# Bucket stage of a two-layer graph network: VectorE's fold of the last bucket is put between the first and the second comparison

## What is computed

```python
h1 = relu(x[row] @ nbW + nbb); h2 = relu(x[col] @ selfW + selfb)
log_alpha = concatenate([h1, h2]) @ attW + attb
gate = sigmoid(log(u) - log1p(-u) + log_alpha)         # u: clipped noise of the edge
mask = clip(gate * (ZETA - GAMMA) + GAMMA, 0, 1)
d = clip((segment_sum(mask, row) + EPS_DEG) ** -0.5, 0, 10)
out = segment_sum((mask * d[row] * d[col])[:, None] * x[col], row)
```

## Time and profile before

| | us |
|---|---|
| median of 3 runs | 5892.25 (5885.24 to 5893.28) |
| the profiled execution's own time | 5890.85 |
| its span in the trace | 5889.1 |
| DVE busy in it | 5129.1 (87%) |
| PE busy in it | 4101.6 (70%) |
| bucket stage, layer 0: first `ids` to last fold | 3342.40 to 3763.41 |
| bucket stage, layer 1 | 5452.88 to 5883.42 |

### The profile page before, as it was taken

How to read it: one execution, slowest core, us unless ns; L and a number is a source line. 1 busy time by engine, 2 the same in 40 slices (tenths; PEclk the granted TensorE clock), 3 DMA queues, 4 the chain that set the end, 5 groups by cost and what they waited for, 6 DMA issues and landing times. The chain is left out here.

```text
span 5889.1 us, 162768 instructions
## 1 busy us (share of the span) xinstructions
PE 4101.6 (70%) x56330; PEld 3657.5 (62%) x56330; DVE 5129.1 (87%) x10832; ACT 2500.9 (42%) x5126; POOL 1164.4 (20%) x1562
## 2 busy tenths in 40 slices
PE   2777777777677888854555477888888725554777
PEld 2666666666445888854444477658888624443676
DVE  8999999999644999989999899509999799999888
ACT  2666666566044555524555200135555325554000
POOL 0000000000000333310000277303333200000776
PEclk9777677777555555556777799755555567777999
DMA  3000000000043666748999799517666579997999
GB/s 73 0 0 0 0 0 0 0 0 0 1 22 130 232 231 233 235 139 305 329 331 330 291 379 378 199 53 233 230 233 230 164 253 330 330 330 281 381 381 348
DMA packets 428687, 1120.74 MB, mean 190 GB/s; under 512 B 206962, under 2 KB 212707, under 8 KB 428023
## 3 DMA queue, kind: packets, MB, share of 16 engines
q1 hardware_dynamic: 316700, 549.97, 29.8%
q0 software_dynamic: 65856, 316.89, 14.2%
q10 hardware_dynamic: 46036, 252.74, 11.3%
HBM read 873.65 MB, written 279.36 MB: 196 GB/s over the span
## 5 line engine op out<-in xcount | busy, mean ns | idle before, releaser
L1611 PE MATMUL psG<-y_window,area 128*128 128x64 bf16 x14976 | 668.2, 217 | 780.4 <-DVE area L1256 665.3
L1611 PEld LDWEIGHTS psG<-y_window,area 128*128 128x128 bf16 x14976 | 624.7, 114 | 824.2 <-issue 504.0
L642 ACT ACTIVATE work<-iota,work 128x149 bf16<-128x149 f32 x2496 | 789.0, 406 | 0.0
L1430 PE MATMUL psG<-area,work 128*128 128x112 bf16 x2496 | 551.1, 390 | 335.4 <-DVE area L978 335.4
L586 POOL DMA_INDIRECT work<-msg_d,widx x396 | 428.3, 1082 | 1655.7 <-issue 1610.4
L1430 PEld LDWEIGHTS psG<-area,work 128*128 128x128 bf16 x2496 | 357.7, 149 | 483.7 <-issue 338.0
L1423 PE MATMUL psG<-work,merge 128*128 128x148 bf16 x4992 | 546.2, 294 | 68.9 <-ACT work L642 68.9
L1624 PE MATMUL psG<-work,edge 128*128 128x192 bf16 x4752 | 447.7, 251 | 202.8 <-DVE edge L1291 202.8
L1423 PEld LDWEIGHTS psG<-work,merge 128*128 128x128 bf16 x4992 | 529.6, 132 | 91.4 <-issue 65.6
L816 ACT ACTIVATE work<-merge 128x1024 bf16<-128x1024 f32 x312 | 330.1, 1058 | 549.4 <-DVE merge L1266 549.4
L1624 PEld LDWEIGHTS psG<-work,edge 128*128 128x128 bf16 x4752 | 412.2, 145 | 238.0 <-DVE edge L1291 163.4
(11 more groups left out here) (268 smaller groups left out, 8280.4 us busy)
## 6 DMA issues: line engine op xcount, KB each, us to landing
msg_d<-work ACTq DMA_DIRECT2D x312, 776.0 KB, 4.5
area<-rlo_d SPq DMA_DIRECT2D x312, 512.0 KB, 4.1
merge<-crel_d SPq DMA_DIRECT2D x312, 512.0 KB, 5.0
area<-crelp_d SPq DMA_DIRECT2D x312, 512.0 KB, 5.6
y_window<-y_d SPq DMA_DIRECT2D x312, 48.0 KB, 3.5
y_d<-cur SPq DMA_DIRECT2D x7, 1008.0 KB, 3.8
y_d<-work SPq DMA_DIRECT2D x7, 1008.0 KB, 4.8
work<-msg_d,widx POOLq DMA_INDIRECT x396, 6.9
```

What stands on the lines that cost most here:

```text
L642: ins = act.activation(below[:, h, k, :], iota_all[:, :], ACT.Sign, bias=keyf[:, bass.ds(t * CT + k, 1)], scale=-1.0)
L1430: ins = pe.matmul(psG[:, 2 + h, 0:RECS * CT], place[:, h, :, k], spread_rec[:, h, :, :, k], start=k == 0, stop=k == CT - 1)
L1611: ins = pe.matmul(psG[:, 2 * h + k // CH, k % CH * D:(k % CH + 1) * D], col_one_hots[:, h, k * P:(k + 1) * P], y_window[:, h, m * D:(m + 1 ...
```

## The change

`bucket_out(b - 1)` is called inside `bucket_hots(b)`, directly behind the first of the three comparisons, instead of in `buckets` behind the third. The very last fold, `bucket_out(HI - 1)`, stays where it was. No instruction is added or dropped, and no wait or semaphore is changed; line numbers behind the edit shift by two (1297 becomes 1299, 1301 becomes 1303, 1303 becomes 1305).

```diff
@@ -1290,6 +1290,8 @@
                     for g in range(WG):
                         dve.tensor_tensor(q_one_hots[s][:, g, :, :], iota_rows,
                                           ids[:, s, g * WIN:(g + 1) * WIN].unsqueeze(1).to_broadcast([P, P, WIN]), ALU.is_equal).then_inc(q_hots_ready, 1)
+                        if g == 0 and (not isinstance(b, int) or b > 0):
+                            bucket_out(b - 1, (s - 1) % SLOTS)
 
                 def bucket_out(b, s):
                     n = L * HI + b
@@ -1311,8 +1313,6 @@
                         b = i * SLOTS + s
                         if not isinstance(b, int) or b < HI:
                             bucket_hots(b, s, L * len(range(s, HI, SLOTS)) + i + 1)
-                            if not isinstance(b, int) or b > 0:
-                                bucket_out(b - 1, (s - 1) % SLOTS)
```

## The result

The changed kernel takes **5942.84 us** (median of 3 runs, 5939.84 to 5946.01) against 5892.25: a ratio of 1.0088, 95% interval 1.0068 to 1.0108. It is slower by 51 us, as forecast (5938, range 5912 to 5975). The profiled execution took 5946.01 with a span of 5944.1.

A forecast was written before the change was run, and what follows sets the result against it. DVE's own chain was taken to bound the kernel, with PE beside it. Loops +23 and +17, ends +2 and +4 made +46 us on 5890.85: 5937, as a median 5938, range 5912 to 5975.

The forecast's parts named there:

- The sum is ready 1.69 after the third comparison: Bucket loops: PE's last 16 products end 1.69 us after the third comparison starts; the fold follows at 1.73, not 1.45.
- DVE stands still for 0.28 in each bucket: Bucket loops: the moved fold waits 0.28 us for PE, some 280 times, about 75 us in all.
- The upper bound: A later second comparison behind the store adds up to 0.13 us a bucket, +36 us, giving 5974.
- A period of 3.02 and 3.04: New time per bucket in us in layers 0 and 1, from 2.85 and 2.92: +23 and +17 us.
- the ends: Outside the steady loops: +2 us for buckets behind the loops, +2 for each layer's first six.
- The branch hides behind two comparisons: At each loop's end: the branch's cost of 0.45 or 0.34 us, once in six buckets, disappears.
- Late loads vanish at the slower pace: Layer 1's loop: late loads, part of its 2.92 us a bucket, have more time at 3.04.
- Loads set the pace: Rival in the bucket loops: the loads, not DVE, give 2.85 and 2.92, so no difference, 5892 us; 6%.
- the faster rival: Bucket loops: the sum is there in time, period 2.76 and 2.74, 37 us less, 5855; 5%.
- PE's clock: Rival in both loops: PE drops to its low clock, period grows by 1.0, 276 us on top, 6214; 3%.
- POOL: Rival in the bucket loops: both issues meet comparisons, 3.40 us a bucket, +142 us, 6037 with the ends; 6%.
- POOL waits more for PE: Sign expected in the loops if the forecast was right: more POOL waiting for PE; no size given.

The follow-up runs named there:

- one-issue run: Changed kernel with one indirect DMA of 22 rows for a bucket in place of two of 16 and 8: 5940.79 us, ratio 1.0080.

## Why the prediction was right, point by point

**The sum is ready 1.69 after the third comparison, and the fold can start at 1.73.** The third comparison starts at 3522.30 - 0.60 = 3521.70. The sum ends at 3523.40, 1.70 later, and the fold starts at 3523.44, 1.74 later. The parts hold too: 0.74 from comparison to product (0.75 worked out), 1.56 for 16 products (1.55), 0.04 to the fold.

**DVE stands still for 0.28 in each bucket, about 75 us in the view.** It is 0.30; the view says 0.23 each and 65.6 us in all, because it counts from the end of the comparison and not from where the next instruction could have started. The number of waits, 286, is the 280 forecast.

**Store to second comparison 0.17 and 0.20.** 3520.93 to 3521.10 in layer 0, and in layer 1 5665.08 to 5665.28. The upper bound built on it wasn't needed.

**A period of 3.02 and 3.04.** Measured 3.04 and 3.08. The sum had 23 + 17 = 40 us for the two loops and they cost 48, so it was short by 8 there; it had 6 for the ends and 3 are left for everything outside the loops. That the total is only 5 us off, 5938 for 5943, is in part this luck. In layer 1 a part of the 8 is one bucket in six whose store comes 0.61 after the fold and not 0.50:

```profile
5664.47 0.36 DVE L1299 TENSOR_REDUCE summed<-psG 128x64 f32<-128x192 f32 x1 [0.23 <-PE psG L1624]
5665.08 0.28 DVE L1305 SCALAR_TENSOR_TENSOR cur<-summed,dinv,cur 128x64 f32 x1 [0.25 <-DVE summed L1299]
5665.28 1.29 DVE L1291 TENSOR_TENSOR merge<-y_edge,ids 128x1024 bf16<-128x1024 int16 x2
```

**The branch hides behind two comparisons.** The waits ahead of `ids` fell from 7.4 us to 0.2 in layer 0. The Trainium skill (Advanced Engine Details and Errata, Sequencer Loop) says that other engine instructions can be read and queued while a control instruction executes. The trace now agrees, with those two comparisons queued ahead of the branch. It was no net gain here, since the new wait for PE costs more.

**Late loads vanish at the slower pace, PEclk stays.** GB/s fell by 6% and 5% and PEclk is 1.00 in the windows of both loops, as forecast. The DMA share was to fall by some 5% too and fell only from 1.00 to 0.98.

**The rivals.** *Loads set the pace* was wrong for this change, since 3.04 is above their pace, but it was right for every order without the wait: the kernels that fold later or older data stop at 5891, where 5855 was worked out. The price of the faster rival left this out. *PE's clock* fell: PE idles 0.70 ahead of its 16 products, and PEclk stays 1.00. *POOL* was wrong as a bound, as its one-issue run shows. *POOL waits more for PE* was wrong as a sign: in 379 us of layer 0 (3361 to 3740) the idle time ahead of its issues that is put down to PE went from 39.3 us to 1.8, because its issues got longer (last section).

## What to carry to other kernels

When a step is moved earlier on its engine, work out when its input is ready from the last piece that the new order makes late, and not from how long it was ready before: the fold had over a microsecond to spare behind the third comparison, 0.4 behind the second and minus 0.3 behind the first. A moved consumer that stands ahead of its own next producer closes a ring through two engines, and everything hidden on the other engine becomes a term of it. And before counting a gain on the bounding engine, look at how close behind it the next resource is: here 0.1 us a bucket of room was already taken by the loads.

## What was not expected of the hardware

**POOL's issues stretch with DVE's comparisons and not with their own work.** One indirect DMA of 22 rows is the same instruction in two of the runs. Groups of layer 0's loop, first with the fold behind the second comparison, then in the changed kernel (busy us, mean ns | idle before):

```profile
L586 POOL DMA_INDIRECT work<-msg_d,widx x91 | 91.9, 1010 | 154.7 <-PE psG L1624 147.9 <-issue 6.8
```

```profile
L586 POOL DMA_INDIRECT work<-msg_d,widx x83 | 118.5, 1427 | 131.3 <-PE psG L1624 127.2 <-issue 4.1
```

1.01 against 1.43 us. In the changed kernel itself POOL has two issues a bucket, of 1.14 and 1.28, and with 0.30 behind each these fill 3.02 of the 3.03 exactly; it looks like a bound and is none, for with one issue the time is the same.

The rows of the changed kernel show why they fill it. The issue at 3521.37 starts while the comparison of 3521.10 runs, which ends 0.69 later, at 3521.79; the issue ends at 3522.65, 0.86 behind that. The next one starts at 3522.96 in the comparison of 3522.53 and ends at 3524.10, 0.88 behind its end at 3523.22. In the whole trace of the changed kernel 554 of the 588 issues start so, more than 0.12 us before the end of a comparison that runs, and nearly all of them end 0.86 to 0.88 us behind that comparison's end; the others last 1.00. So an issue is tied to a comparison of DVE, and POOL's length follows DVE's period. An issue that starts just before a comparison isn't stretched: in the rows of the kernel with the fold behind the second comparison, 3522.11 (0.99) beside 3522.14. The Trainium skill (SBUF — State Buffer, Who interferes with whom) says that a VectorE instruction with two SBUF inputs contends with a GpSimd instruction that reads SBUF; the comparisons are such instructions, and these rows agree.

**A DMA share near 1.00 doesn't say that the DMA engines are the limit.** The same indirect DMA of 22 rows, in the line of its queue in layer 0 (3361 to 3740), first with the fold behind the second comparison, then in the changed kernel:

```profile
q0 software_dynamic: 20014, 151.81, 98.8%
```

```profile
q0 software_dynamic: 18094, 137.25, 98.2%
```

Packets of the same mean size, 7.6 KB, and nearly the same share, but 401 GB/s in the one and 362 in the other, where the wait for PE sets the pace and each packet just takes longer. The share tells how long packets were under way, not how many bytes could have gone in that time.
